# Local attention scores in tiles of 64 rows, keys masked by head on GpSimd, and the agents' rows loaded by a broadcast

## The reference

```python
x = _layernorm(x + _L0_attn_ref(x, ...))    # agents: one row of 256 per batch, times a token factor
x = _layernorm(x + _L0_xattn_ref(x, ctx, ctx, ...))   # one head, 361 keys
x = _layernorm(x + _L0_ffn_ref(x, ...))     # 50 of the 100 tokens by a gate, 16 heads of 16
x = _layernorm(x + _L1_attn_ref(x, ...))    # local attention, 16 heads of 16, band of +-64
x = _layernorm(x + _L1_xattn_ref(x, ctx, ctx, ...))
x = _layernorm(x + _L1_ffn_ref(x, ...))     # quantized linear layer

# _L0_attn_ref ends in
return agent_tok * agent_v[:, None, :]      # agent_v: 32 x 256, softmax over one element is agent_tok
# _L1_attn_ref
scores = jnp.einsum('bhtd,bhtwd->bhtw', q, kb) / scaling
scores = jnp.where(valid[None, None], scores, -jnp.inf)
probs = jax.nn.softmax(scores, axis=-1)
ctx = jnp.einsum('bhtw,bhtwd->bhtd', probs, vb)
```

## Time and profile before

| | |
|---|---|
| median of 3 runs (lowest to highest) | 1149.96 us (1148.42 to 1151.2) |
| the profiled execution | 1141.62 us |
| its span, first to last instruction | 1139.5 us |
| mean granted TensorE clock | 0.861 of full speed |

### The profile page before, as it was taken

The page is one execution under the profiler, slowest core; times in us unless marked ns, Lnnn a source line. Parts: engine busy times, 40 slices in busy tenths (PEclk is TensorE's granted clock), DMA queues, the critical chain, the costliest instruction groups (busy, mean ns, idle before and its releaser), DMA issues.

```text
span 1139.5 us, 19498 instructions
## 1 busy us (share of the span) xinstructions
PE 963.4 (85%) x6958; PEld 706.0 (62%) x6958; DVE 705.2 (62%) x2131; ACT 542.9 (48%) x2440; POOL 315.8 (28%) x460
## 2 busy tenths in 40 slices
PE   6887988989787999886798799899899889998774
PEld 4665776656565766664476586466557666665552
DVE  4226675457787765535777755365848875556664
ACT  3112446667334257654434436556534345675431
POOL 0045211133542220403442320033344330122231
PEclk9857999879898899887889897688679798899676
DMA  7904100002221000010213000002201200000000
GB/s 206 279 22 134 36 2 1 1 21 81 83 89 70 15 1 2 22 54 28 77 40 122 16 1 2 1 22 75 76 28 55 70 15 1 1 2 1 8 8 15
DMA packets 21429, 50.78 MB, mean 45 GB/s; under 512 B 3376, under 2 KB 9236, under 8 KB 21332
## 3 DMA queue, kind: packets, MB, share of 16 engines
q1 hardware_dynamic: 21332, 49.53, 13.3%
HBM read 46.25 MB, written 3.28 MB: 43 GB/s over the span
## 4 chain that ended last, share of the span: by engine, by line
PE 52%; DVE 23%; ACT 17%; issue 3%; POOL 2%; DMA 1%; SPq 1%; DVEq 0%; POOLq 0%
PE psum L419 8%; PE psum L458 8%; ACT work L779 8%; PE psum L424 6%; ACT work L738 5%; PE psum L590 5%; PE psum L444 4%; DVE bn L896 4%; PE psum L604 3%; DVE x L903 2%; PE psum L596 2%; PE psum L610 2%; DVE res L944 1%; DMA ctxT<-in_x 1%; PE psum L414 1%
## 5 line engine op out<-in xcount | busy, mean ns | idle before, releaser
L779 ACT ACTIVATE work<-psum,mx 100x100 f32<-100x100 f32 x512 | 169.9, 381 | 63.3 <-DVE mx L1052 63.1
L779 ACT ACTIVATION_READ_ACCUMULATOR work<-psum,mx 100x1 f32 x512 | 124.6, 245 | 0.0
L1138 POOL TENSOR_SCALAR ve<-mv 100x2 f32<-100x2 f32 x96 | 22.4, 233 | 335.3 <-DVE mv L898 335.1
L458 PE MATMUL psum<-eT,ctx 128*128 128x100 f32 x768 | 102.9, 291 | 3.6 <-DVE eT L932 3.5
L458 PEld LDWEIGHTS psum<-eT,ctx 128*128 128x128 f32 x768 | 99.5, 207 | 6.5 <-DVE eT L932 5.1
L604 PE MATMUL psum<-ident,work 100*100 100x100 f32 x512 | 75.7, 285 | 30.8 <-ACT work L779 30.3
L444 PE MATMUL psum<-ctxT,qT 128*100 128x361 f32 x256 | 91.2, 502 | 5.1 <-ACT qT L669 2.9
L669 ACT ACTIVATE eT<-psum 100x400 f32<-100x400 f32 (+3 forms) x128 | 66.3, 532 | 45.6 <-PE psum L451 21.8
L604 PEld LDWEIGHTS psum<-ident,work 100*100 100x100 f32 x512 | 57.1, 148 | 47.9 <-ACT work L779 43.4
L590 PE MATMUL psum<-kT,qT 32*100 32x200 f32 x512 | 84.5, 410 | 2.7 <-DVE aT L1067 2.4
L1052 DVE TENSOR_REDUCE mx<-psum 100x4 f32<-100x400 f32 x128 | 66.9, 565 | 32.0 <-PE psum L596 31.4
(11 more groups left out here) (234 smaller groups left out, 2184.4 us busy)
## 6 DMA issues: line engine op xcount, KB each, us to landing
ctx<-in_ctx SPq DMA_DIRECT2D x16, 768.0 KB, 6.4
ctxT<-in_ctxT SPq DMA_DIRECT2D x16, 722.0 KB, 4.3
cell<-in_cell SPq DMA_DIRECT2D x16, 282.0 KB
seq<-in_seq SPq DMA_DIRECT2D x16, 282.0 KB
x<-in_x SPq DMA_DIRECT2D x16, 200.0 KB
out<-xplus SPq DMA_DIRECT2D x16, 200.0 KB
work<-in_x SPq DMA_DIRECT2D x4, 400.0 KB
ctx<-in_x SPq DMA_DIRECT2D x2, 400.0 KB
```

The lines of the kernel that those rows point to most:

```text
L458: last = e.matmul(bk[b][:, c * S:(c + 1) * S], s.ctx[:, b, j, c * P:(c + 1) * P], s.pT[:, b, j, :], start=j == 0, stop=j == S2C - 1)
L779: last = e.activation(s.e[:, h, :], bk[g][0:S, q * S:(q + 1) * S], ACT.Exp, bias=s.mx[0:S, h:h + 1], accum_out=s.den[0:S, h:h + 1])
```

## The change

Scores: GpSimd writes the keys of a unit into `keys` as four copies of 100 columns, each with all but one of four heads zeroed by `heads` (128 x 400 values, two buffers in turn, the room of kT). One matmul of 64 rows and 400 columns per bank then gives four heads' scores, with one edge matmul of 280 columns per bank. kT is replaced by `kall`, both halves with their bias, written by VectorE; ScalarE's two kT copies go, and VectorE takes over one of the two copies of v. v is stored in 32 columns per head, 16 of them zero, so eight matmuls of 100 columns in pairs that accumulate leave each head's result in its place, and ScalarE's masked copy and VectorE's masked add go; ScalarE copies the transposed reciprocals instead, which are now made before the value matmuls. The agents' matmul goes: `agent_v` is written to DRAM once and a DMA with a broadcast fills 100 partitions of the upper part of `eT` for each turn. All five strings of `ORDER` are new.

```diff
-                    for wave in range(2):
-                        if wave:
-                            e.wait_ge(*pe(f"hs{i}", t))
-                        for g in range(2):
-                            r = 32 * (2 * wave + g)
-                            last = e.matmul(bk[g][0:S, wave * T:(wave + 1) * T], s.qT[r:r + 32, c, b * S:(b + 1) * S],
-                                            s.kT[r:r + 32, :, c, b * S:(b + 1) * S], start=wave == 0, stop=False,
-                                            skip_group_check=True)
...
+                    e.wait_ge(*pool(f"bd{i}", t))
+                    for g in range(2):
+                        r = 64 * g
+                        e.matmul(bk[g][0:S, 0:4 * S], s.qT[r:r + 64, c, b * S:(b + 1) * S], s.keys[r:r + 64, i % 2, :, :],
+                                 start=True, stop=False, skip_group_check=True)
+                    for g in range(2):
+                        last = e.matmul(edges(bk[g]), band_w[:, :],
...
+                    e.wait_ge(*dve(f"eT{i}", t))
+                    e.wait_ge(*pool(f"re{i}", t))
+                    e.transpose(bk[1][:, 0:S], s.rspread, ident[0:S, 0:S]).then_inc(*pe.up(f"R{i}"))
                     e.wait_ge(*act(f"eT{i}", t))
-                    e.wait_ge(*dve(f"eT{i}", t))
-                    for r in range(ROWS):
-                        e.matmul(bk[0][32 * r:32 * r + 32, 0:T], s.v[0:S, b, c * P + 32 * r:c * P + 32 * r + 32],
-                                 s.eT[0:S, r * T:(r + 1) * T], start=True, stop=True)
-                    e.wait_ge(*pool(f"re{i}", t))
-                    e.transpose(bk[1][:, 0:S], s.rspread[0:S, 0:P], ident[0:S, 0:S]).then_inc(*pe.up(f"av{i}"))
+                    for j in range(2):
+                        for r in range(ROWS):
+                            h = 2 * r + j
+                            last = e.matmul(bk[0][32 * r:32 * r + 32, 0:S], s.v[0:S, b, c * HQ + h, :],
+                                            s.eT[0:S, h * S:(h + 1) * S], start=j == 0, stop=j == 1, skip_group_check=True)
...
-                for b in range(NB):
-                    if t:
-                        e.wait_ge(*s.vector["quant"](f"r{b}", t - 1))
-                    n = NB * s.pair(t) + b
-                    e.matmul(bk[b][0:S, 0:D], ident[0:B, n:n + 1].to_broadcast([B, S]), agent_v[:, :],
-                             start=True, stop=True).then_inc(*pe.up(f"agv{b}"))
...
-                    e.scalar_tensor_tensor(s.xT[:, 1, 0:S], bk[0][:, S:2 * S], own[:, 1:2], s.xT[:, 0, 0:S], ALU.mult,
-                                           ALU.add).then_inc(*dve.up(f"u{i}"))
...
         def gpsimd_agents(e):
             e.wait_ge(*agent_pe("u7"))
-            e.wait_ge(*agent_dve("w8"))
             for s in streams:
                 last = e.memset(s.work[32 * (ROWS - 1):P, 0:H * HALF], 0.0)
...
+            e.wait_ge(*agent_dve("w8"))
+            e.wait_ge(*agent_pe("yT2"))
             for s in streams:
-                last = e.memset(s.v_pick[:, :, :, :], 0.0)
+                e.memset(s.v_pick[:, :, :, :], 0.0)
+                last = e.memset(s.v[:, :, :, :], 0.0)
...
+            def blocks(t, i):
...
+                else:
+                    e.wait_ge(*s.tensor["local"](f"s{i - 2}", t))
+                e.tensor_tensor(s.keys[:, i % 2, :, :], s.kall[:, c, b * S:(b + 1) * S].unsqueeze(1).to_broadcast([P, 4, S]),
+                                heads[:, :].unsqueeze(2).to_broadcast([P, 4, S]), ALU.mult).then_inc(
+                    *s.gpsimd["local"].up(f"bd{i}"))
...
+            e.wait_ge(*agent_dve("v"))
+            e.dma_start(agent_rows.rearrange("n (b d) -> (n b) d", b=NB), agent_v).then_inc(agent_kept, 16)
+            e.wait_ge(agent_kept, 16)
+            for s in streams:
+                load_agent(e, s, 0)
...
                     load_ctx(e, s, t + 1)
+                    load_agent(e, s, t + 1)
...
-            e.wait_ge(*agent_pool("zeros"))
+            e.wait_ge(*agent_pool("rows"))
...
     "SP": (
-        "ABCCDDABCAABADBABCDCCDDBACABABDBACCDCDDBCABAABDBCCDCDDBACD"),
+        "ABCDCDABACAABDBABCDCCDDBAAACDBBBACCDCDDBAAACDBBBDCCCDDCABD"),
```

More of the change, by code:

```diff
@@ L68 @@
 TENSOR = {
-    "mix": "agv0 agv1",
     "first": "xT q s0 s1 pT0 pT1 av0 av1 out0 out1",
     "pick": "gates selT gath q k v hs0 hs tr0 tr1 av fo sc0 sc1",
-    "local": "xT q k0 k1 v0 v1 " + " ".join(f"hs{i} s{i} tra{i} trb{i} av{i}" for i in range(NB * NC)) + " out0 out1",
+    "local": "xT q k v0 v1 " + " ".join(f"s{i} tra{i} trb{i} R{i} av{i}" for i in range(NB * NC)) + " out0 out1",
     "second": "xT q s0 s1 pT0 pT1 av0 av1 out0 out1",
@@ L79 @@
     "pick": "ez selT xT q vs0 ex0 ex1 eT0 rT fo",
-    "local": "xT q k1 v0 v1 " + " ".join(f"exa{i} exb{i} eT{i} u{i}" for i in range(NB * NC)),
+    "local": "xT q v0 " + " ".join(f"exa{i} exb{i} eT{i} R{i}" for i in range(NB * NC)),
     "second": "xT q cb0 cb1 ex0 ex1 pT1 aT0",
@@ L88 @@
     "pick": "z0 z1 gp gt dg0 dg1 tie0 rk0 tie1 rk1 pk0 pk1 kT vs1 mx0 mx1 rd eT1 aT " + NORM,
-    "local": "k0 " + " ".join(f"ma{i} mb{i} rd{i} eT{i} u{i} aT{i}" for i in range(NB * NC)) + " " + NORM,
+    "local": "k0 k1 v1 " + " ".join(f"ma{i} mb{i} rd{i} eT{i} aT{i}" for i in range(NB * NC)) + " " + NORM,
     "second": "mx0 nb0 mx1 nb1 pT0 rs aT1 " + NORM,
@@ L97 @@
     "pick": "re ve rstd",
-    "local": "xb " + " ".join(f"re{i}" for i in range(NB * NC)) + " ve rstd",
+    "local": "xb bd0 " + " ".join(f"bd{i + 1} re{i}" for i in range(NB * NC - 1)) + f" re{NB * NC - 1} ve rstd",
     "second": "xb prod qb ve rstd",
@@ L467, in tensor_turns @@
             for t in range(TURNS):
-                pe, act, dve, pool = s.at("mix")
-                for b in range(NB):
-                    if t:
-                        e.wait_ge(*s.vector["quant"](f"r{b}", t - 1))
-                    n = NB * s.pair(t) + b
-                    e.matmul(bk[b][0:S, 0:D], ident[0:B, n:n + 1].to_broadcast([B, S]), agent_v[:, :],
-                             start=True, stop=True).then_inc(*pe.up(f"agv{b}"))
-                yield
-                yield from cross(t, "first", dve, W["x_k"], W["x_o"])
+                yield from cross(t, "first", s.vector["mix"], W["x_k"], W["x_o"])
                 pe, act, dve, pool = s.at("pick")
@@ L545, in tensor_turns @@
                 for c in range(NC):
-                    last = e.transpose(bk[1][:, c * P:(c + 1) * P], s.rspread[:, c * P:(c + 1) * P], ident[:, :])
+                    last = e.transpose(bk[1][:, c * P:(c + 1) * P], s.rspread_pick[:, c * P:(c + 1) * P], ident[:, :])
                 last.then_inc(*pe.up("av"))
@@ L763, in scalar_turns @@
                 yield
-                e.wait_ge(*pe("k1", t))
-                for j in range(2):
-                    last = e.activation(s.kT[:, j, 1, :], bk[1][:, 0:T], ACT.Identity, scale=own[:, j:j + 1],
-                                        bias=bkh[:, j, 1:2])
-                last.then_inc(*act.up("k1"))
+                e.wait_ge(*pe("v0", t))
+                copy(padded(s.v[0:S, 0, :, :]), bk[1][0:S, 0:D].rearrange("p (n j d) -> p n j d", j=2, d=DH)).then_inc(
+                    *act.up("v0"))
                 yield
-                for b in range(NB):
-                    e.wait_ge(*pe(f"v{b}", t))
-                    copy(s.v[0:S, b, :], bk[b][0:S, 0:D]).then_inc(*act.up(f"v{b}"))
-                    yield
                 for i in range(NB * NC):
@@ L1042, in vector_turns @@
                 pe, act, dve, pool = s.at("local")
-                e.wait_ge(*pe("k0", t))
-                for j in range(2):
-                    last = e.tensor_scalar(s.kT[:, j, 0, :], bk[0][:, 0:T], own[:, j:j + 1], bkh[:, j, 0:1], ALU.mult, ALU.add)
-                last.then_inc(*dve.up("k0"))
+                e.wait_ge(*pe("k", t))
+                for h in range(NC):
+                    e.tensor_scalar(s.kall[:, h, :], bk[0][:, h * T:(h + 1) * T], cols["a_bk"][:, h:h + 1], None,
+                                    ALU.add).then_inc(*dve.up(f"k{h}"))
+                yield
+                e.wait_ge(*pe("v1", t))
+                e.tensor_copy(padded(s.v[0:S, 1, :, :]), bk[0][0:S, 0:D].rearrange("p (n j d) -> p n j d", j=2, d=DH)).then_inc(
+                    *dve.up("v1"))
                 yield
@@ L1257, in sync_first @@
             e.dma_start(wscale[:, :], ins["wscale"].to_broadcast([P, 1])).then_inc(ld_const, 16)
-            for n, tile in (("ident_b", ident_b), ("before", before), ("own", own), ("band_w", band_w), ("band_x", band_x)):
+            for n, tile in (("ident_b", ident_b), ("before", before), ("own", own), ("heads", heads), ("band_w", band_w), ("band_x", band_x)):
                 e.dma_start(tile[:, :], ins[n]).then_inc(ld_const, 16)
```

212 lines of the change are left out of this document (112 added, 100 removed).

## The result

The changed kernel takes 1080.56 us (median of 4 runs, 1077.02 to 1081.76) where the kernel before takes 1150.58 beside it (1148.42 to 1156.68): a ratio of 0.9378, 95% interval 0.9335 to 0.9421. The profiled execution has a span of 1079.9 us.

What follows compares the result with a forecast made beforehand. TensorE was taken as nearest to a bound (85% busy, 52% of the chain), not proven. Terms -16.5 - 10 - 8 - 5 + 4.5 + 2 + 4 - 5 = -34 us took 1149.96 to 1116 us, range 1094 to 1142.

Steps and rivals of the forecast that it cites:

- -5 us for the end: Last stages of streams C and D: the new string lets them end together, waiting beside each other; -5 us.
- the +4 of the start: Program start: zeroing the value buffers and loading the agents' rows delay stream A's transposes from 79.4 to 83.2 us; +4 us.
- The chain's quotients: Worth of a microsecond taken from an engine, chain time over busy time: TensorE 0.62, VectorE 0.37, ScalarE 0.36, GpSimd 0.07.
- the second rival: Scores: pairs of 64 rows do not run side by side, giving 1151 us, no change; chance 0.07.
- the scores' cost of 16.5 us: Scores in one wave: 0.31 us less per unit, 20 us over 64 units, at quotient 0.83 a saving of 16.5 us.
- The sign for the agents' loads: Check on the agents' DMA: no VectorE idle time before L963 that a DMA ended, except at the start.
- The maskings' worth: 64 maskings on GpSimd, 1.0 us each: 64 us at 0.07, +4.5 us, plus +2 us for stalls of VectorE.
- the second term of "GpSimd against VectorE": VectorE beside GpSimd: stalls cost +2 us; the agents' L963, reading both inputs from SBUF, becomes one more that can be stalled.
- The first, TensorE as the bound throughout: Rival: TensorE's 36 us count whole and bring their idle share, 42 us, giving 1097 us; chance 0.18.
- The fourth: Rival: new strings put waits at the head of TensorE's queue that eat half the gain, 1133 us; chance 0.10.
- GpSimd's price: Rival: maskings delay GpSimd's queue, up to 64 us on the path, break-even 40 us, at worst 1174 us; chance 0.10.
- The check of the prediction: TensorE's share of the span should stay at 84 or 85%; below 82% the forecast is wrong, time having gone into waits.

Runs made afterwards that it cites:

- agents_load: Kernel before with only the agents' rows changed to a DRAM write and broadcast loads, TensorE's 64 matmuls for them gone: ratio 0.9943 to the kernel before.
- two_waves: Changed kernel with each unit's scores again in two waves of 32 rows and 200 columns, edges behind each: ratio 0.9553 to the kernel before.
- new_code_retuned: Changed kernel's code with strings re-tuned by a model of the queues, starting from the adapted old strings: ratio 0.9424 to the kernel before.
- new_code_old_strings: Changed kernel's code with the strings of the kernel before, missing steps put in and vanished ones removed: ratio 0.9905 to the kernel before.

## Why the prediction was wrong

**The step that failed** is the account of the strings. The forecast valued all five at -5 us for the end and priced everything else, the +4 of the start with it, as if the queues stayed as they were: -33 + 4 = -29 us. With the queues as they were, the new code measured -11 us; the new strings then brought 61 us more (0.9905 - 0.9378 of 1150) and on the old code nothing. So both parts of the sum were off, the first too large and the second far too small, and the right sign of -34 supports neither. The chain's quotients didn't tell what freed time is worth here: with the old strings 44 of 49 us came back as idle time. The spans of the new code with old and new strings, 54.2 us apart, split without a rest: TensorE's idle time falls by 40.2 us (219.7 to 179.5), and its busy time by 14.0 (914.4 to 900.4) for the same matmuls at a higher clock. The start came as forecast, A's transposes at 83.06 us (83.2), though the mask sum was done at 77.3 us and not at 81.2. At the end TensorE has 4 us more work in the last 40 us, which fits the -5; neither was tried apart.

**The parts that were right, one by one.** The edges 0.84 us behind the scores (0.84), a unit's 1.22 us (1.23), so pairs of 64 rows run side by side and the second rival is out; the scores' cost of 16.5 us under the new strings (16.6 to 20; under the old ones 27); the agents' rows with their start, -6 us (-6.6); the value matmuls at nothing (L610's 39.4 us are now 39.2 at L599). The maskings took 0.85 us, not 1.0, GpSimd 371 us, not 380, and the normalization's mean stayed at 504 ns. The sign for the agents' loads holds for those loads; two waits of VectorE ahead of L945, 6.7 us in all and late in the program, ended with the load of x.

**Mis-sized.** The maskings' worth, some 22 us if a masking costs what a second one does, where 6.5 were in the sum: the quotient from the chain, 0.07, says how often GpSimd was last, not what it costs VectorE and the clock (0.40 measured, for a second masking). ScalarE lost 29 us where the sum had 22, since the copy of the reciprocals, put at the same size, takes 263 ns and the masked one took 365. VectorE was to lose 13 us and lost nothing. The masked add's 19.9 us are gone, but the copies of v cost 6.7, L945 takes 650 ns in the mean where L963 took 469, and others are longer too (the normalization into `xplus` 617 ns where it took 525). L963 never took over 484 ns; L945 takes 475 in the median and up to 1919, here beside an operation of GpSimd:

```profile
92.16 1.92 DVE L945 SCALAR_TENSOR_TENSOR res<-eT,tok,x 100x256 f32<-100x256 f32 x1
92.08 1.71 POOL L1162 TENSOR_TENSOR kT<-cell,kT 100x722 f32<-100x722 f32 x1 [1.31 <-ACT cell L665]
```

That is the stall of which the second term of "GpSimd against VectorE" spoke, and agents_load has it (609 ns) with no masking at all, so it comes with the agents' operand in SBUF. The Trainium skill (SBUF — State Buffer, two separate sides) says that a GpSimd operation that reads SBUF and a VectorE operation with two SBUF inputs exclude each other for a whole instruction, and the trace agrees: L945 started 0.08 us after GpSimd's and ended 0.29 us after it.

**TensorE's time.** It fell by 63 us and not 38. At the old strings' clock (0.863 against 0.861) the code takes 49, and the new strings 14 more. Of the 49 the forecast's terms had 36. Its 20 us for the scores were distances at the full clock, where two_waves shows 22 in the mean over both clocks; for the agents it left out the 7.1 us at the start. The last 4 us are a remainder that no line was found for.

**The rivals.** The first, TensorE as the bound throughout (1097 us), came nearest and still fell short by 16. Its premise, that removed work brings its share of idle time along, is not what happened: idle time stayed at 176 to 180. The fourth, that the new strings put waits at the head of the queue, did not happen on balance; the like of it is seen with the old strings on the new code (44 of 49 us are idle time again), and the new ones undid it. GpSimd's price, 22 us by a second masking, is a third of what its rival needed at worst (64) and half of its break-even (40). The check of the prediction, TensorE's share below 82%, did not fire at 83%, since it couldn't tell a kernel whose busy time and span fall together.

**What stays open.** Why the same 7022 instructions of TensorE are granted 0.863 in one order and 0.906 in another (and the same 7406 0.837 to 0.874) is not settled by any run; no edit here changes the clock alone. The sum of the parts is not the gain either: undone together under the new strings, three parts and the copies give back 56 us with the maskings still there, while the old code with these strings has lost all 70. What the other 15 are (value matmuls, agents, the start, or the positions of the steps put in) was not tried apart.

## What to carry to other kernels

Where hand-made or searched strings set the queues, price a change of code and its strings together: the changed code with the old strings is one experiment and says what the rest depends on (here 11 of 70 us). The busiest engine's idle time stayed between 162 and 190 us in 15 of the 20 kernels of the table; it was more in new_code_retuned and in the four with less work than their strings were made for. With strings that fit, most of its removed work counted: the scores' 22 us of busy time were worth 17 to 20. Take that work at the mean clock and not at the full one. A quotient read from the chain prices neither a helper engine that stalls its neighbour nor parts that lean on the same slack; doubling the added operation gives an estimate of its price.

## What the runs showed of the hardware

The same 7022 instructions of TensorE took between 882.6 us and 914.4 us by order alone, at mean granted clocks of 0.906 and 0.863. That is more than executions of one kernel differ: the four of new_code_retuned had 0.893 to 0.906, of the changed kernel 0.874 to 0.879, of new_code_old_strings 0.853 to 0.863. The page and the clock of new_code_retuned, to be read beside those of new_code_old_strings:

```profile
PE 882.6 (81%) x7022; PEld 652.4 (60%) x7022; DVE 711.2 (66%) x2081; ACT 514.1 (47%) x2392; POOL 369.2 (34%) x528
```

```profile
core 0: 1083.7 us, clock 0.906
```

It had more idle time than the changed kernel (201 against 180 us) and gained it back by the clock, so fewer idle microseconds are not by themselves a higher clock. The Trainium skill (TensorE: Matmul & The Clock Gate, Part 1) says that the clock follows how busy TensorE has just been; against the changed kernel the clock and the idle total rose together here, which would fit if it counts where the idle time lies. These runs suggest that and don't isolate it.
